# Three order tables of a four-layer graph kernel are replaced, with the sums of VectorE inside SBUF placed apart from GpSimd's long instructions

## The chip, the core and the metric

The kernel runs on one core of a Trainium2 chip. A core has five engines with queues of their own: TensorE (PE in the profile; its weight loads are PEld), VectorE (DVE), ScalarE (ACT), GpSimd (POOL) and SyncE (SP), which here issues every DMA. Each engine works through its queue in order, and engines wait for each other only through semaphores. SBUF is the memory that all of them read and write, PSUM the eight banks that TensorE writes into. The metric is the time of one execution on the device, in microseconds (us); lower is better.

## The reference

The input is 64 graphs of 128 nodes with 256 features, x [64, 128, 256], and a sparse adjacency adj [64, 128, 128]. Four layers follow each other, each with a residual and a layer norm:

```
w = adj * exp(q @ k^T); y = (w / rowsum(w)) @ v        # layer 0; q, k, v from x
x = layernorm(x + y)
h = relu(adj @ (x @ W1) + b1); h = relu(adj @ (h @ W2) + b2)
x = layernorm(x + adj @ (h @ W3) + b3)                 # layer 1
# layer 2: H = (adj != 0); conv(z, W) = Dn * (H @ (Be * (H^T @ (z @ W^T)))) + b
h = norm512(relu(conv(x, Wup))) * gamma + beta
x = layernorm(x + (conv(h, Wdown) + x))
# layer 3: 8 heads of 32, scores times (adj + adj), softmax, context, Wo
x = layernorm(x + mha(x, adj))
```

All is float32; the kernel's products with weights are made of float32r halves ("high" and "rest"), whose three products are added in PSUM.

## The kernel before

Four graphs form a group; there are 16 groups, g = 0 to 15. A group passes four stages, A (layer 0 and most of layer 1), T (the end of layer 1), B (layer 2) and C (layer 3), and several groups are in flight at a time, each in another stage. So while TensorE does the softmax products of group g - 3, it does the up projection of g - 2 and the attention of g.

What stands in what order is written in three tables. PROLOGUE lists (step, group) for each engine until the pipeline is full, SCHEDULE lists (stage, step) for one loop round, which runs 11 times, and EPILOGUE lists the rest. `run` walks through them. A step is a function of an engine: `mha_shift` of DVE is the subtraction of the row maximum from a graph's scores, and each step waits for the semaphores of what it reads. Where a step overwrites a bank or a tile that is still read, and the order doesn't already give it, there is a further wait whose count ("due") stands in a small dictionary in the step.

The steps that the prediction speaks of:
- x0's norm. DVE computes the row statistics (`x0_means`, L1306, and `x0_stats`, L1315 and L1317), GpSimd raises the variance to the power -1/2 (L1579), DVE scales (`x0_norm`, L1322), and TensorE's `gcn_ax` reads the result. x1, x2 and x3 have the same chain.
- `mha_shift3` (L1495): DVE adds the negated row maxima to graph 3's scores, both from SBUF. `mha_max` (L1491) reads the scores alone. `mha_scores` (L1486) takes the scores out of PSUM and multiplies them by adjB. ACT then takes the exponentials, GpSimd divides (`mha_div`, L1628), TensorE turns the result (`mha_turn`), ACT and DVE copy one half each (L1513 on DVE).
- `square_sum0` and `square_sum1` (L1455, L1459, L1462): DVE adds up four tiles of squares of layer 2's hidden values, from SBUF; TensorE transposes the sum in `hyper_down`.
- `mha_wo` on DVE (L1526): x3 = product in PSUM + x2. TensorE's `mha_turn3` writes its bank only after the first of these.
- `incidence` (L1407 to L1416): a compare of adjT with zero, a sum of rows, a reciprocal and a product.
- `hyper_rest` and `mha_xt` (L1301) are the "rest" halves of the up projection's and of qk's input. `rest_W...` (L1295) are those of the weights, made once. `hyper_up01` of group 0 waits for the rests of WupT, W3, Wv3T and WoT.
- On GpSimd: `up_rest` (L1612), `x_rest` (L1633), `att_t` (L1588, x plus a bias row), `x0_bias` (L1601), `x2_bias` (L1624), each a sum over 128x1024.
- On SyncE: `next_xT`, `next_x`, `gcn_3a1` (loads the adjT of the group after next), `mha_scores1` (loads the next adjB, once the masks have used the old one), `x3_norm0` and `x3_norm1` (store half of a result each, after DVE's scaling of it).

Of the kernel before, what the change touches and what calls it, by code (L numbers as in the profile page):

```python
# [55 lines left out]
def width(weights):  # L56
# [7 lines left out]
    "PE": [("set_att", 0), ("set_vec", 0), ("keep_busy2", 0), ("att_t", 0), ("att_t_rest", 0), ("keep_busy5", 0),  # L64
        ("set_down", 0), ("set_wo", 0), ("att_scores", 0), ("att_v0", 0), ("att_v1", 0), ("att_t", 1), ("att_v0", 1),
        ("att_out", 0), ("att_t_rest", 1), ("att_v1", 1), ("gram", 0), ("att_scores", 1), ("gcn_ax", 0), ("att_out", 1),
# [211 lines left out]
def build(nc, A):  # L278
# [1407 lines left out]
```

## Time and profile before

| | us |
|---|---|
| median of 3 runs | 1079.01 (1076.88 to 1079.46) |
| the profiled execution | 1078.44 |
| its span, first to last instruction | 1076.6 |
| PE busy | 1011.8 (94%) |
| DVE busy | 880.3 (82%) |
| ACT busy | 641.7 (60%) |
| POOL busy | 499.5 (46%) |
| one row maximum on DVE (L1491), mean | 1.20 |
| one copy of half a turn on DVE (L1513), mean | 0.68 |
| one load of adjT, issue to landing, median | 3.6 |

The profile is one execution. Busy is the time in which an engine had at least one instruction; the idle time ahead of an instruction is put down to the semaphore that came last. The granted clock of TensorE is given as a share of its full rate; in the profiled run it was 0.984 on average. The DMA queues moved 36 GB/s on average.

### The profile page before, as it was taken

Reading aid. Unit: us, or ns where it says so; the run is one execution under the profiler, and the core shown is the slowest. Engines: PE = TensorE matmul, PEld = TensorE weight load, DVE = VectorE, ACT = ScalarE, POOL = GpSimd, SP = SyncE. Lnnn points to the kernel's source line nnn. Section 1 sums busy time; section 2 is a strip of 40 time slices with the busy share of each in tenths; the row PEclk is TensorE's granted clock in tenths of the full one; section 3 lists DMA queues with packets and bytes.
Section 4 is the critical chain, followed back from the end, with each engine's and each line's share of the span. In section 5 each row is a group of like instructions: output and inputs, shape, how many; then the busy total and the mean of one; then the engine's idle time right before and its main releaser. Section 6 shows DMA issues by size and latency. Waiting matters only on the chain.

```text
span 1076.6 us, 21459 instructions
## 1 busy us (share of the span) xinstructions
PE 1011.8 (94%) x8252; PEld 900.9 (84%) x8252; DVE 880.3 (82%) x2252; ACT 641.7 (60%) x1739; POOL 499.5 (46%) x298
## 2 busy tenths in 40 slices
PE   7997999999999999999999999999999999988877
PEld 6896889888888988988898898888888887977665
DVE  5875798988879788888978889798888979787887
ACT  2564394755738476483846738385673838458274
POOL 3413456362734536173363626436372554418243
PEclk8998999999999999999999999999999999999988
DMA  6101010201001010010101001010100100010001
GB/s 255 40 30 40 11 51 1 80 1 50 30 21 60 11 63 8 24 57 11 69 2 50 31 21 60 11 69 2 50 31 21 59 12 21 1 41 1 1 11 50
DMA packets 15078, 39.14 MB, mean 36 GB/s; under 512 B 1792, under 2 KB 1792, under 8 KB 14848
## 3 DMA queue, kind: packets, MB, share of 16 engines
q1 hardware_dynamic: 14976, 37.77, 9.9%
q8 instruction: 65, 1.06, 0.4%
q14 instruction: 37, 0.30, 0.1%
HBM read 29.38 MB, written 8.39 MB: 35 GB/s over the span
## 4 chain that ended last, share of the span: by engine, by line
PE 64%; DVE 22%; ACT 5%; issue 4%; POOL 3%; DMA 0%; POOLq 0%; DVEq 0%; SPq 0%
PE ps L638 59%; POOL rstd L1579 3%; DVE x L1368 2%; DVE st L1306 2%; PE ps L1018 2%; DVE x L1322 2%; DVE hT L1434 2%; DVE sqs L1459 2%; DVE fT_rest L1301 2%; PE ps L947 1%; ACT aT_high L1116 1%; ACT ps L1118 1%; ACT upT L1165 1%; DVE sqs L1462 1%; PE ps L929 1%
## 5 line engine op out<-in xcount | busy, mean ns | idle before, releaser
L1628 POOL TENSOR_TENSOR pr<-pr,den 128x1024 f32<-128x1024 f32 x60 | 114.8, 1914 | 254.8 <-DVE den L1509 254.7
L1579 POOL TENSOR_TENSOR rstd<-var,neg_half 128x4 f32<-128x4 f32 (+1 forms) x84 | 83.9, 999 | 170.1 <-DVE var L1317 169.9
L1180 ACT ACTIVATE pr<-pr,mx 128x128 f32<-128x128 f32 x360 | 140.1, 403 | 7.3 <-DVE mx L1491 7.3
L1133 ACT COPY s_s<-ps 128x512 f32<-128x512 f32 x30 | 17.6, 587 | 138.6 <-PE ps L638 138.6
L1486 DVE TENSOR_TENSOR pr<-ps,adjB 128x1024 f32<-128x1024 f32 x60 | 70.5, 1216 | 20.1 <-PE ps L638 20.1
L1322 DVE TENSOR_SCALAR x<-x,mv,rstd 128x256 f32<-128x256 f32 x184 | 66.5, 418 | 22.2 <-POOL rstd L1579 21.9
L1612 POOL TENSOR_TENSOR up_rest<-upT,up_high 128x1024 fp32r<-128x1024 f32 x30 | 73.0, 2432 | 12.2 <-ACT upT L1160 12.2
L1180 ACT ACTIVATION_READ_ACCUMULATOR pr<-pr,mx 128x1 f32 x360 | 72.3, 201 | 0.0
L1174 ACT ACTIVATE qkT<-ps,biases 128x512 f32<-128x512 f32 x60 | 37.1, 689 | 57.0 <-PE ps L638 56.8
L1491 DVE TENSOR_REDUCE mx<-pr 128x8 f32<-128x1024 f32 x60 | 70.9, 1200 | 0.0
L1306 DVE BATCH_NORM_STATS2 st<-x 128x6 f32<-128x256 f32 x184 | 66.1, 412 | 0.2
L638 PE MATMUL ps<-W_high,aT_high 128*128 128x256 f32 x240 | 65.9, 298 | 0.0
L1018 PE MATMUL ps<-ident,pr 128*128 128x128 f32 x480 | 61.1, 275 | 5.1 <-DVE x L1526 5.1
L638 PE MATMUL ps<-WdownT_high,up_high 128*128 128x258 f32 x240 | 62.0, 290 | 0.7 <-DVE x L1526 0.7
L1513 DVE COPY pr<-ps 128x512 f32<-128x512 f32 x60 | 39.4, 676 | 28.2 <-PE ps L1018 28.2
L1018 PEld LDWEIGHTS ps<-ident,pr 128*128 128x128 f32 x480 | 54.0, 141 | 10.1 <-issue 7.9
L638 PE MATMUL ps<-W_rest,aT_high 128*128 128x256 f32 x240 | 62.2, 282 | 0.0
L638 PE MATMUL ps<-WdownT_rest,up_high 128*128 128x258 f32 x240 | 60.4, 283 | 0.0
L638 PE MATMUL ps<-fT_high,WupT_high 128*128 128x512 f32 x120 | 50.7, 422 | 5.4 <-DVE WoT_rest L1295 5.4
L1156 ACT ACTIVATE up_high<-ps,biases 128x512 fp32r<-128x512 f32 x60 | 41.3, 689 | 19.8 <-PE ps L638 19.7
L1301 DVE TENSOR_TENSOR fT_rest<-ps,fT_high 128x512 fp32r<-128x512 f32 x60 | 38.5, 681 | 15.1 <-ACT fT_high L1170 14.1
L1617 POOL TENSOR_TENSOR hv<-hv,neg_half 128x2 f32<-128x2 f32 x32 | 23.0, 718 | 60.2 <-DVE hv L1450 60.2
(336 smaller groups left out, 3411.0 us busy)
## 6 DMA issues: line engine op xcount, KB each, us to landing
xT<-in_xT SPq DMA_DIRECT2D x15, 512.0 KB, 3.2
x<-in_x SPq DMA_DIRECT2D x15, 512.0 KB, 3.4
out_x<-x SPq DMA_DIRECT2D x30, 256.0 KB, 2.0
adjT<-in_adjT SPq DMA_DIRECT2D x16, 256.0 KB, 3.6
adjB<-in_adj SPq DMA_DIRECT2D x15, 256.0 KB, 3.3
pr<-in_weights SPq DMA_DIRECT2D x2, 512.0 KB, 6.3
qkT<-in_weights SPq DMA_DIRECT2D x1, 1024.0 KB, 13.4
upT<-in_weights SPq DMA_DIRECT2D x1, 768.0 KB, 10.7
```

Of the source, the lines that this page charges most:

```text
L638: return pe.matmul(out, lhsT, rhs, start=(k == 0), stop=(k == n - 1))
L1018: last = pe.transpose(ps4[:, turn_bank(g, b) + k // 4, k % 4], pr_of(g)[:, b, k, :], ident[:])
L1156: act.activation(up_high_of(g)[:, f, :], ps[:, up4(g) + f, :], ACT.Relu, bias=b_up[:, f, :]).then_inc(up_high_ready, 1)
L1180: act.activation(pr_of(g)[:, b, k, :], pr_of(g)[:, b, k, :], ACT.Exp, bias=mx[ended(g)][:, b, k:k + 1], accum_out=den[ended(g)][:, b, 0, k ...
L1301: dve.tensor_tensor(part_rest[:, c, :], ps[:, bank + c, :], high_part[:, c, :], ALU.subtract).then_inc(ready, 1)
L1306: dve.bn_stats(st[norm(i, g)][:, b, :], t[:, b, :]).then_inc(norm_step[i], 1)
L1322: dve.tensor_scalar(t[:, b, :], t[:, b, :], mv[norm(i, g)][:, b, 0:1], rstd[norm(i, g)][:, b:b + 1], ALU.subtract, ALU.mult).then_inc(read ...
L1486: dve.tensor_tensor(pr_of(g)[:, b].rearrange("p (j i) n -> p j i n", i=C), ps4[:, up4(g):up4(g) + 4, 2 * bb:2 * bb + 2, :], mask, ALU.mult ...
L1491: dve.tensor_reduce(mx[ended(g)][:, b, :], pr_of(g)[:, b], AX.X, ALU.max, negate=True).then_inc(mx_ready, 1)
L1579: pool.tensor_tensor(rstd[norm(i, g)][:, bs], var[norm(i, g)][:, bs], neg_half[:, bs], ALU.pow).then_inc(rstd_ready[i], len(pairs))
L1612: pool.tensor_tensor(up_rest_of(g)[:, fs, :], upT_of(g)[:, fs, :], up_high_of(g)[:, fs, :], ALU.subtract).then_inc(up_rest_ready, 1)
L1628: pool.tensor_tensor(pr_of(g)[:, b], pr_of(g)[:, b], den[ended(g)][:, b, 1, :].unsqueeze(2).broadcast_to([P, HEADS, P]), ALU.mult).then_in ...
```

## The change

All three tables are new. No step is dropped or added. In the loop, steps of a stage moved across the round's border, so that some are listed under another stage letter (the same group of graphs all the same). Besides that the due counts of bank and tile waits are written anew for the new order. Here are the lines of the tables that hold the shift and WoT's rest, and most of the due counts:

```diff
@@ PROLOGUE, DVE
-        ("gram_scale", 2), ("gcn_ax1", 2), ("gcn_ax", 2), ("rest_WoT", 0), ("x1_stats0p", 1), ("x1_means1", 1),
...
+        ("gcn_3a1", 0), ("x1_stats0p", 0), ("rest_WoT", 0), ("x1_norm0p", 0), ("rest_WdownT", 0), ("x1_means1", 0),
...
@@ SCHEDULE, DVE
-        ("N", "x0_means0"), ("N", "x0_means1"), ("N", "x0_stats"), ("B", "mha_shift3"), ("N", "x0_norm")],
...
+        ("A", "degrees"), ("C", "mha_shift3"), ("A", "gram_scale"), ("C", "mha_div2"), ("C", "mha_turn1"),
...
@@ PE: att_t, gcn_1, gram_turn
-                        due = {(1, 1): 0, (1, 2): 0}.get((m, g), {1: 1 * g}.get(m, 0))
+                        due = {(1, 1): 0, (1, 2): 1}.get((m, g), {1: 1 * g}.get(m, 0))
...
-                due = {0: 0}.get(g, 2 * g + 2)
+                due = {1: 0, 2: 0}.get(g, 2 * g + 2)
                 if due > 0:
                     pe.wait_ge(gm_ready, due)
...
-                due = {0: 1, 1: 0, 2: 0, 3: 7, 15: 0}.get(g, 2 * g + 2)
+                due = {0: 1, 2: 5}.get(g, 0)
                 if due > 0:
                     pe.wait_ge(z2_rest, due)
@@ PE: hyper_down_high
                 pe.wait_ge(up_high_ready, HC * g + HC)
+                due = {(0, 1): 0, (0, 13): 0, (0, 14): 0, (0, 15): 0}.get((half, g), {0: 4 * g}.get(half, 0))
+                if due > 0:
+                    pe.wait_ge(prT_act, due)
@@ ACT: gram_turn, hyper_x
-                due = {2: 0, 15: 0}.get(g, 2 * g - 2)
+                due = {2: 2}.get(g, 0)
                 if due > 0:
                     act.wait_ge(hyper_done, due)
...
+                due = {1: 2, 14: 28}.get(g, 0)
+                if due > 0:
+                    act.wait_ge(v3_done, due)
@@ DVE: mha_wo
-                due = {(0, 15): 0}.get((pair, g), {0: 16 * g}.get(pair, 0))
+                due = {(0, 13): 208}.get((pair, g), 0)
                 if due > 0:
                     dve.wait_ge(out_stored[0], due)
```

The first place is x0's norm on VectorE in a loop round. Before, from the statistics of x0 (x_100) on, with `pr` the scores, `mx_124` the maxima, `dn_109` the degrees and `hT` the scaled Gram matrix:

```order
L1306 BN_STATS st_131<-x_100 128x6 x4
L1313 MEMSET held 128x1
L1315 BN_AGGR mv_139<-st_131 128x2 x4
L1317 TENSOR_REDUCE var_147<-mv_139 128x4
L1495 TENSOR_TENSOR pr<-pr,mx_124 128x1024
L1322 TENSOR_SCALAR x_100<-x_100,mv_139,rstd_155 128x256 x4
L1423 TENSOR_SCALAR dn_109<-ps 128x4
L1424 TENSOR_SCALAR dn_109<-ps 128x4
L1426 SCALAR_TENSOR_TENSOR dn_109<-ps,dn_109 128x4
L1428 RECIPROCAL dn_109<-dn_109 128x4
L1322 TENSOR_SCALAR x_odd<-x_odd,mv_140,rstd_156 128x256 x4
L1434 TENSOR_SCALAR hT<-ps,dn_109 128x128 x4
```

Now the same stretch (the line numbers are 19 higher):

```order
L1325 BN_STATS st_131<-x_100 128x6 x4
L1332 MEMSET held 128x1
L1334 BN_AGGR mv_139<-st_131 128x2 x4
L1336 TENSOR_REDUCE var_147<-mv_139 128x4
L1510 TENSOR_REDUCE mx_124<-pr 128x8
L1341 TENSOR_SCALAR x_100<-x_100,mv_139,rstd_155 128x256 x4
L1442 TENSOR_SCALAR dn_109<-ps 128x4
L1443 TENSOR_SCALAR dn_109<-ps 128x4
L1445 SCALAR_TENSOR_TENSOR dn_109<-ps,dn_109 128x4
L1447 RECIPROCAL dn_109<-dn_109 128x4
L1514 TENSOR_TENSOR pr<-pr,mx_124 128x1024
L1453 TENSOR_SCALAR hT<-ps,dn_109 128x128 x4
```

The shift went from ahead of x0's scaling to ahead of hT, the last row maximum came into its place, and x1's scaling (x_odd) left this stretch.

The second place is the squares on VectorE, later in the same round; `sqs` is their sum, `x_130` is x3, `aT_rest` a rest half. Before:

```order
L1513 COPY pr<-ps 128x512
L1386 TENSOR_TENSOR aT_rest<-ps,aT_high 128x512 x2
L1455 TENSOR_TENSOR sqs<-upT 128x512
L1526 TENSOR_TENSOR x_130<-ps,x_121 128x512
L1513 COPY pr<-ps 128x512
L1306 BN_STATS st_134<-x_130 128x6 x2
L1313 MEMSET held 128x1
L1315 BN_AGGR mv_142<-st_134 128x2 x2
L1317 TENSOR_REDUCE var_150<-mv_142 128x2
L1396 TENSOR_TENSOR ctx_rest<-ps,ctxT 128x512
L1459 TENSOR_TENSOR sqs<-sqs,upT 128x512
L1462 TENSOR_TENSOR sqs<-sqs,upT 128x512
```

Now:

```order
L1545 TENSOR_TENSOR x_130<-ps,x_121 128x512
L1332 MEMSET held 128x1
L1334 BN_AGGR mv_140<-st_132 128x2 x4
L1336 TENSOR_REDUCE var_148<-mv_140 128x4
L1532 COPY pr<-ps 128x512
L1325 BN_STATS st_134<-x_130 128x6 x2
L1332 MEMSET held 128x1
L1334 BN_AGGR mv_142<-st_134 128x2 x2
L1336 TENSOR_REDUCE var_150<-mv_142 128x2
L1341 TENSOR_SCALAR x_odd<-x_odd,mv_140,rstd_156 128x256 x4
L1474 TENSOR_TENSOR sqs<-upT 128x512
L1478 TENSOR_TENSOR sqs<-sqs,upT 128x512
```

The first sum of squares no longer stands ahead of x3's sum; all three now stand together behind x1's scaling, and the third is followed by ctx_rest.

The third place is SyncE's queue in the loop; `out_x<-x_130` is half a store of x3. Before:

```order
L602 DMA xT<-in_xT 128x1024
L617 DMA adjB<-in_adj 128x512
L606 DMA x<-in_x 128x1024
L612 DMA adjT_81<-in_adjT 128x512
L626 DMA out_x<-x_130 128x512 x2
```

Now:

```order
L604 DMA xT<-in_xT 128x1024
L628 DMA out_x<-x_130 128x512
L614 DMA adjT_81<-in_adjT 128x512
L628 DMA out_x<-x_130 128x512
L619 DMA adjB<-in_adj 128x512
L608 DMA x<-in_x 128x1024
```

The loads of adjT, adjB and x, which stood ahead of both halves of the store, now stand behind the first half or behind both.

## Rows read from the trace of the kernel before

**Rows 1.** The page, part 1: busy us (share of the span), instructions of each engine.

```profile
PE 1011.8 (94%) x8252; PEld 900.9 (84%) x8252; DVE 880.3 (82%) x2252; ACT 641.7 (60%) x1739; POOL 499.5 (46%) x298
```

**Rows 2.** Busy time by stretch: PE, PEld, DVE, ACT, POOL; PEclk; DMA.

```profile
0.00:98.73 98.73, 84.67 (x518) 75.72 (x519) 67.48 (x224) 45.40 (x97) 29.06 (x23) 0.93 0.27 99
...
225.86:861.66 635.80, 616.28 (x5122) 551.73 (x5121) 536.62 (x1371) 395.07 (x1080) 312.01 (x181) 1.00 0.10 34
...
925.00:1076.60 151.60, 126.59 (x1134) 109.21 (x1132) 118.58 (x269) 81.70 (x237) 61.12 (x40) 0.94 0.05 19
92.40:98.70 6.30, 6.30 (x18) 4.98 (x19) 2.19 (x7) 1.66 (x3) 0.00 (x0) 0.62 0.00 0
1025.60:1040.00 14.40, 13.61 (x68) 11.70 (x69) 10.81 (x18) 11.47 (x42) 5.34 (x4) 0.76 0.03 13
```

**Rows 3.** Waits of PE, whole kernel: total us, times, longest.

```profile
PE ps L638 <- DVE x L1322: 12.9, 12, 2.9
PE ps L638 <- DVE WoT_rest L1295: 5.4, 1, 5.4
PE ps L638 <- DMA pr<-in_weights: 5.4, 1, 5.4
PE ps L1018 <- DVE x L1526: 5.1, 11, 0.5
...
PE ps L638 <- DVE fT_rest L1301: 3.0, 11, 0.3
PE ps L638 <- DVE pr L1513: 2.7, 1, 2.7
PE ps L638 <- DVE att_rest L1295: 2.4, 1, 2.4
...
PE ps L638 <- DVE hT L1434: 2.1, 11, 0.2
```

**Rows 4.** The same from 225.86 to 861.66, ten loop periods.

```profile
PE ps L638 <- DVE x L1322: 8.7, 10, 0.9
```

**Rows 5.** In order of time: start us, us; POOL and DVE in a loop period.

```profile
606.27 2.41 POOL L1612 TENSOR_TENSOR up_rest<-upT,up_high 128x1024 fp32r<-128x1024 f32 x1
607.39 1.84 DVE L1455 TENSOR_TENSOR sqs<-upT 128x512 f32<-128x512 f32 x1 [0.27 <-ACT upT L1165]
608.64 2.82 POOL L1601 TENSOR_TENSOR x<-x,rows 128x1024 f32<-128x1024 f32 x1
...
657.05 1.22 DVE L1495 TENSOR_TENSOR pr<-pr,mx 128x1024 f32<-128x1024 f32 x1
657.28 1.85 POOL L1579 TENSOR_TENSOR rstd<-var,neg_half 128x4 f32<-128x4 f32 x1 [1.31 <-DVE var L1317]
```

**Rows 6.** L1455's shortest, median and longest ns; a power met by nothing.

```profile
L1455 DVE TENSOR_TENSOR sqs<-upT x15: 681/1835/2755, 106.0 to 985.5; 128x512 f32<-128x512 f32 x15
...
1006.01 1.02 POOL L1579 TENSOR_TENSOR rstd<-var,neg_half 128x4 f32<-128x4 f32 x1 [2.60 <-DVE var L1317]
```

**Rows 7.** In order of time, ACT: the two copies of aT.

```profile
661.74 1.06 ACT L1111 CAST aT_high<-ps 128x512 fp32r<-128x512 f32 x2
```

**Rows 8.** The tail in order of time: DVE's two sums of x2, PE's turn.

```profile
1019.66 1.27 DVE L1474 SCALAR_TENSOR_TENSOR x<-x_odd,ps 128x512 f32<-128x512 f32 x2
...
1025.71 0.69 PE L947 MATMUL ps<-ident,x 128*128 128x128 f32 x2 [4.74 <-DVE x L1322]
```

**Rows 9.** In order of time, PE: four matmuls of qk.

```profile
634.20 1.07 PE L638 MATMUL ps<-fT_rest,Wqk3T_high 128*128 128x512 f32 x4
```

**Rows 10.** In order of time, DVE: qk's rests, the masks of group and graph pair.

```profile
632.69 1.29 DVE L1301 TENSOR_TENSOR fT_rest<-ps,fT_high 128x512 fp32r<-128x512 f32 x2 [1.12 <-ACT fT_high L1170]
...
640.61 2.35 DVE L1486 TENSOR_TENSOR pr<-ps,adjB 128x1024 f32<-128x1024 f32 x2 [1.21 <-PE ps L638]
```

**Rows 11.** The loads of adjB, 15 of them.

```profile
DMA to landing us min/median/max: 2.7/3.3/5.3
```

**Rows 12.** The compare of the incidence: shortest, median and longest ns.

```profile
L1407 DVE TENSOR_SCALAR hT<-adjT x15: 408/417/1190, 9.2 to 888.7; 128x512 f32<-128x512 f32 x15
```

More of the change, by code:

```diff
@@ L134 @@
-    "POOL": [("x_rest", 0), ("att_t", 0), ("att_t", 1), ("x_rest", 1), ("x0_stats0p", 0), ("x0_stats1p", 0),
[7 rows of a table removed]
-    "SP": [("next_x", 2), ("next_xT", 2), ("gcn_3a1", 0), ("next_xT", 3), ("gcn_3a1", 1), ("next_x", 3),
-        ("first_adjB", 0), ("gcn_3a1", 2), ("next_xT", 4), ("mha_scores1", 0), ("next_x", 4), ("x3_norm1", 0),
-        ("x3_norm0", 0)],
+    "PE": [("keep_busy5", 0), ("set_att", 0), ("keep_busy2", 0), ("att_t", 0), ("set_vec", 0), ("att_t_rest", 0),
+        ("set_wo", 0), ("set_down", 0), ("att_scores", 0), ("att_t", 1), ("att_t_rest", 1), ("att_v0", 0),
+        ("att_v1", 0), ("att_v0", 1), ("att_out", 0), ("att_v1", 1), ("gram", 0), ("att_scores", 1), ("gcn_ax", 0),
[6 rows of a table added]
+        ("gram_turn", 1), ("gram", 2), ("hyper_x", 0), ("gcn_ax", 2), ("hyper_up01", 0), ("hyper_up01_rest", 0),
[12 rows of a table added]
+        ("hyper_out", 1), ("gram_turn", 3), ("gcn_3s1", 3), ("att_t", 4), ("gcn_3a0", 3), ("att_t_rest", 4),
+        ("mha_xt", 1), ("gcn_3a1", 3), ("mha_qk01", 1), ("mha_qk01_rest", 1), ("mha_qk2", 1), ("mha_qk3", 1)],
@@ new lines @@
+    "DVE": [("set_reps", 0), ("set_rep", 0), ("set_att", 0), ("rest_att", 0), ("incidence", 0), ("set_vec", 0),
+        ("set_down", 0), ("rest_Wv0T", 0), ("rest_W1", 0), ("set_wo", 0), ("incidence", 1), ("att_exp", 0),
+        ("att_out", 0), ("att_res1", 0), ("x0_means0", 0), ("x0_stats0p", 0), ("x0_means1", 0), ("x0_stats1p", 0),
+        ("x0_norm0p", 0), ("degrees", 0), ("x0_norm1p", 0), ("att_exp", 1), ("gram_scale", 0), ("gcn_ax", 0),
[24 rows of a table added]
+    "ACT": [("x_high", 0), ("high_att", 0), ("high_W3", 0), ("high_W2", 0), ("x_high", 1), ("att_t", 0),
+        ("high_Wv0T", 0), ("high_W1", 0), ("high_WoT", 0), ("att_t", 1), ("att_v0", 0), ("att_v1", 0), ("att_off", 0),
+        ("att_exp", 0), ("high_Wqk3T", 0), ("att_v0", 1), ("att_v1", 1), ("att_off", 1), ("att_exp", 1), ("gcn_ax", 0),
+        ("gcn_1", 0), ("gcn_2s0", 0), ("gcn_2s1", 0), ("gcn_2a", 0), ("gcn_ax", 1), ("high_WupT", 0), ("gcn_1", 1),
+        ("gcn_3s0", 0), ("gcn_3s1", 0), ("x_high", 2), ("gcn_2s0", 1), ("gcn_2s1", 1), ("high_Wv3T", 0),
+        ("high_WdownT", 0), ("gram_turn", 0), ("gcn_2a", 1), ("att_v0", 2), ("att_t", 2), ("att_v1", 2), ("att_off", 2),
+        ("att_exp", 2), ("gcn_3s0", 1), ("gcn_3s1", 1), ("gram_turn", 1), ("hyper_x", 0), ("gcn_ax", 2), ("x_high", 3),
[9 rows of a table added]
@@ L145 @@
+    "POOL": [("att_t", 0), ("x_rest", 0), ("att_t", 1), ("x_rest", 1), ("x0_stats0p", 0), ("x0_stats1p", 0),
[7 rows of a table added]
+    "SP": [("next_xT", 2), ("next_x", 2), ("gcn_3a1", 0), ("gcn_3a1", 1), ("next_xT", 3), ("first_adjB", 0),
+        ("next_x", 3), ("gcn_3a1", 2), ("next_xT", 4), ("x3_norm1", 0), ("x3_norm0", 0), ("mha_scores1", 0),
+        ("next_x", 4)],
 }
 SCHEDULE = {
[3 rows of a table removed]
[1 row of a table added]
         ("A", "att_scores"), ("C", "mha_v1"), ("B", "hyper_x"), ("A", "att_out"), ("B", "hyper_up01"),
@@ L734, in att_v @@
                     if b == 0:
-                        due = {(0, 0, 2): 1, (0, 0, 3): 5}.get((pair, b, g), 0)
+                        due = {(0, 0, 2): 1, (0, 0, 4): 7}.get((pair, b, g), 0)
                         if due > 0:
@@ L745, in att_v @@
                     elif b == 2:
-                        due = {(1, 2): 4 * g + 1}.get((pair, b), 0)
+                        due = {(1, 2, 3): 0}.get((pair, b, g), {(1, 2): 4 * g + 1}.get((pair, b), 0))
                         if due > 0:
@@ L749, in att_v @@
                     else:
-                        due = {(1, 3): 4 * g + 2}.get((pair, b), 0)
+                        due = {(1, 3, 3): 0}.get((pair, b, g), {(1, 3): 4 * g + 2}.get((pair, b), 0))
                         if due > 0:
@@ L768, in att_out @@
                     if b == 0:
-                        pass
+                        due = {(0, 3): 1}.get((b, g), 0)
+                        if due > 0:
+                            pe.wait_ge(v3_ready, due)
                     elif b == 1:
-                        due = {(1, 3): 0}.get((b, g), {1: 2 * g - 4}.get(b, 0))
+                        due = {(1, 3): 0, (1, 15): 0}.get((b, g), {1: 2 * g - 4}.get(b, 0))
                         if due > 0:
@@ L979, in mha_v @@
                     pe.wait_ge(masked_ready, due)
-                due = {(0, 0): 13, (1, 0): 14}.get((pair, g), 0)
+                due = {(1, 0): 14}.get((pair, g), 0)
                 if due > 0:
                     pe.wait_ge(res0_ready, due)
-                due = {(0, 0): 0, (0, 13): 0, (0, 14): 0, (0, 15): 0, (1, 0): 0, (1, 13): 0, (1, 14): 0, (1, 15): 0}.get((pair, g), {0: 4 * g + 15, 1: 4 * g + 16}.get(pair, 0))
+                due = {(0, 13): 31, (1, 13): 32}.get((pair, g), 0)
+                if due > 0:
+                    pe.wait_ge(res1_ready, due)
+                due = {(0, 13): 0, (0, 14): 0, (0, 15): 0, (1, 0): 0, (1, 12): 0, (1, 13): 0, (1, 14): 0, (1, 15): 0}.get((pair, g), {0: 4 * g + 15, 1: 4 * g + 16}.get(pair, 0))
                 if due > 0:
@@ L1007, in mha_turn @@
                 pe.wait_ge(pr_ready, GB * g + b + 1)
+                due = {(2, 14): 58}.get((b, g), 0)
+                if due > 0:
+                    pe.wait_ge(prT_act, due)
+                due = {(2, 14): 58}.get((b, g), 0)
+                if due > 0:
+                    pe.wait_ge(prT_dve, due)
                 due = {3: 2 * g + 1}.get(b, 0)
@@ L1013, in mha_turn @@
                     pe.wait_ge(up_ready, due)
-                due = {(1, 14): 30, (1, 15): 32}.get((b, g), 0)
+                due = {(1, 14): 30}.get((b, g), 0)
                 if due > 0:
@@ L1033, in mha_bias @@
             def mha_bias(g, pair):
-                due = {(0, 15): 61, (1, 15): 63}.get((pair, g), 0)
+                due = {(0, 15): 61}.get((pair, g), 0)
                 if due > 0:
@@ L1085, in att_t @@
                     act.wait_ge(t_done, 2 * g + m + 1)
+                    due = {(0, 0): 1}.get((m, g), 0)
+                    if due > 0:
+                        act.wait_ge(vec_ready, due)
                     act.activation(tT_of(g)[:, m, :], ps[:, low(g) + 1 - m, :], ACT.Identity, bias=t0[:, m:m + 1]).then_inc(t_ready, 1)
@@ L1150, in hyper_x @@
                 act.wait_ge(gx_done, g + 1)
+                due = {1: 2, 14: 28}.get(g, 0)
+                if due > 0:
+                    act.wait_ge(v3_done, due)
                 for c in range(C):
@@ L1156, in up_out @@
                 act.activation(up_high_of(g)[:, f, :], ps[:, up4(g) + f, :], ACT.Relu, bias=b_up[:, f, :]).then_inc(up_high_ready, 1)
-                due = {(2, 0): 1}.get((f, g), 0)
-                if due > 0:
-                    act.wait_ge(rest_ready["WoT"], due)
                 act.activation(upT_of(g)[:, f, :], ps[:, up4(g) + f, :], ACT.Relu, bias=b_up[:, f, :]).then_inc(up_ready, 1)
@@ L1516, in mha_wo @@
                 dve.wait_ge(wo_done, 2 * g + pair + 1)
-                due = {(0, 15): 0}.get((pair, g), {0: 16 * g}.get(pair, 0))
+                due = {(0, 13): 208}.get((pair, g), 0)
                 if due > 0:
                     dve.wait_ge(out_stored[0], due)
-                due = {(1, 12): 192, (1, 13): 208, (1, 14): 224}.get((pair, g), 0)
+                due = {(1, 13): 208, (1, 14): 224}.get((pair, g), 0)
                 if due > 0:
```

11 lines of the change are left out of this document (removed), and 334 rows, old and new, of tables (EPILOGUE, PROLOGUE, SCHEDULE).

## The prediction

> **What bounds the kernel now.** I read the page first, then busy times by stretch, then TensorE's waits, then the instructions around them in order of time. TensorE (PE) is busy 1011.8 us of a span of 1076.6, VectorE (DVE) 880.3 [rows 1], so at most 64.8 us can be won by order alone. The profiled execution took 1078.44, that is 1.8 more than its span and 0.6 less than the median of 1079.01. By stretch [rows 2], PE stands still for 14.1 us in the first 98.7, for 19.5 in the ten loop periods from 225.86 to 861.66 (63.58 us each) and for 25.0 in the last 151.6. Some of this can't go: 5.4 us at the start wait for the first weights [rows 3], and the last sum, norm and store stand behind the last matmul.
>
> Four waits come back in every loop period. Over the whole kernel they are, for the norm of x0 (L1322, ahead of gcn_ax) 12.9 us, for x3's sum (L1526, ahead of the fourth turn) 5.1, for fT's rest 3.0 and for hT 2.1, together 23.1 [rows 3]. In the ten periods the first is 0.87 each [rows 4] and the others by their count and longest 0.5, 0.3 and 0.2: 1.9 of the 1.95 us that PE stands still in a period.
>
> Behind two of them is one thing. At 607.39 the sum of squares L1455 starts on DVE while GpSimd (POOL) is in an up_rest that ends at 608.68 [rows 5]. It takes 1.84 us, where the shortest of its line takes 0.68 [rows 6], and it ends 0.55 us after POOL's instruction, as if it had stood until then. POOL's next, started at 608.64 while the sum still ran, takes 2.82, where the up_rest, of the same size, takes 2.41. The sum of x3 (L1526) stands behind this L1455 on DVE. At 657.05 it is the other way round: DVE starts the shift L1495 (two inputs in SBUF, 1.22 us); POOL's power L1579 is released at 657.28 and takes 1.85 [rows 5] instead of 1.02 [rows 6], and x0's scaling waits for that power, and PE for the scaling.
>
> **The change part by part.** The tables add and remove no instruction; each keeps its duration, unless two of these meet.
>
> *x0's norm in the loop.* The shift goes behind the norm and the degrees. The row maximum of graph 3, one input and 1.2 us, takes its place between variance and scaling; before it stood ahead of att_out. The power takes 1.02 instead of 1.85, 0.8 us less, and the chain starts up to 1.1 earlier since the maximum is out of its way: x0 is ready 1.9 us earlier against a wait of 0.87. Next late would be gcn_1. With 1.4 us less of waits ahead of it PE comes to it at about 662.3; ACT's two copies of aT run from 661.74 to 662.80 [rows 7], and the second is wanted 0.4 us behind the first. I put 0 to 0.4 us a period at that.
>
> *The squares.* Their sums go behind x1's norm, at a place where POOL's next instruction waits for hv, so nothing runs on POOL: 0.7 each instead of 1.84 for the first. Ahead of x3's sum there is now a turn's copy (0.7), so it ends about 1.2 us earlier, against a wait of 0.5. By my walk along the queues the squares are done 0.8 us before PE's transposes want them, the thinnest cover in the loop.
>
> *fT's rest and hT* come 1.1 us earlier with the maximum gone, against waits of 0.3 and 0.2; in front of hT x1's norm (1.35) is replaced by the shift (1.22).
>
> Loop sum, over the kernel: between 0 (every wait replaced by another) and 23.1. I take 21.0, near the upper end, as each wait has at least its own length ahead of it in the walk; 2 us stay for gcn_1.
>
> *Prologue.* PE stands 5.4 us before hyper_up01 of group 0 for WoT_rest [rows 3]. In the new table that sum stands behind gcn_3a1 of group 0, two graph stages earlier, and nothing that I see holds it. Behind the wait PE's granted clock was 0.62 for 6.3 us [rows 2]; at full clock that work takes 3.9, so 2.4 more go with the wait. att_rest moves ahead of the incidence, and PE waits 2.4 for it [rows 3]; POOL's x_rest comes later in turn, behind x's bias, so I count 1.0 of that. Together 8.8. Against it, two more rests stand ahead of group 1 on DVE. I take 8; ends 0 and 14.1, all of the stretch.
>
> *Epilogue.* The longest waits are 4.74 for x2's norm of group 15 [rows 8] and 2.7 for a turn's copy [rows 3], which stood behind a square of 2.75 us, the longest of L1455 [rows 6]. hyper_out of 15 now goes ahead of most of qk and the scores of 14, and its norm ahead of 14's masks. From the sums at 1019.66 to PE's start at 1025.71 are 6.05 us, 1.1 of them a maximum that leaves this place [rows 8]: 4.9. Meanwhile PE has 16 matmuls of 512 columns, four of which take 1.07 with a pitch of 0.23 [rows 9], 3.6 us, and the scores. About 1 us of the 4.74 is left. Behind the old wait the clock was 0.76 for 14.4 us [rows 2], which costs 3.5. With 3.7, 3.5 and 2 of the 2.7 the sum is 9.2; as the tail is a chain as much as a load, I take 8; ends -3 (a newly woven tail has new waits, as long as the turn's) and 14.
>
> The two clock terms are from the rows alone. The Trainium skill (TensorE: Matmul & The Clock Gate, Part 1) says that the gate follows how busy the array has been, with half and full rate as its only levels. The rows at 0.62 and 0.76 behind the two long waits agree, as means over both. By that rule the ends gain 5.9 us beyond their waits if these get short, and nothing if they stay long enough to drop the clock; the sum above goes by the first.
>
> *Dues* (the diff's other lines): the new ones name work that the walk has done 1 us or more before. I put them at 0, upper end 0.4 a period, as for gcn_1.
>
> *SyncE.* The next adjT is now loaded behind the store of x3's first half, adjB and x behind that of the second, which waits for x3_norm1. In the clock of a period of before: fT's rests end at 633.98 [rows 10], x3_norm1 follows until 634.6, and after two issues adjB's load starts at 635.4. Its loads land after 2.7 to 5.3 us, median 3.3 [rows 11], so at 638.7. The masks want it at 640.61, where DVE even waited 1.21 for PE [rows 10]. It is hidden with 1.9 us, and at 5.3 just so. I cost it at nothing.
>
> In sum 21 + 8 + 8 = 37. I hold back 4 for waits that the walk misses. 1078.4 - 33 = 1045.4, and with the 0.6 to the median: 1046.
>
> The skill has a rule that speaks against the change (SBUF — State Buffer, "Who interferes with whom"): not only sums of two SBUF inputs but also compares and copies in the two-port mode fight with GpSimd. The row: L1407, the compare of the incidence, takes 0.42 and once 1.19 [rows 12]. A POOL sum of 2.4 us beside it in the new order would cost DVE up to 2.4 a period by that rule; the room before the masks is about as long, so the sum stays, and the third rival below would decide earlier.
>
> **The rivals.**
> - *Only the loop gains* (0.22): the ends keep their length, as their waits move along their chains. For it: in the last stretch DVE is busy 118.6 of 151.6 us and PE 126.6 [rows 2], neither to the full. Against it: PE's longest waits there have named causes that move. 1079 - 21 + 2 = 1060.
> - *The waits move on* (0.07): in each period PE finds gcn_1's inputs, the squares' or a bank late; 1.85 becomes 1.2, over 11 periods 7 us, and the ends give 4: 1079 - 7 - 4 = 1068. For it: the thin covers of 0 to 0.8 us above.
> - *The loads come late* (0.06, the slower side): adjB waits behind x3_norm1, and each us beyond 640.6 stops the masks, then PE, in 11 periods. A landing of 10 us is 4.8 late, so 53 us, against 33 won: 1099. It decides from a landing of 8.2 us on. Against it: 5.3 is the longest so far.
> - *It doesn't do what it says* (0.03): the sums meet POOL as often as before; 1079.
>
> **How the numbers follow.** The forecast has 0.62 and its own range of 1037 to 1055; the other four hold 0.38. All but the last two are faster: faster 0.91, within 0.3% (about 3 us, what a measurement can tell from no change) 0.03, slower 0.06. The range for eight in ten goes from 1036, where the loop gives its 23 and both ends 10, to 1066, which takes in the second case and leaves out most of the third.
>
> **What would show it.** A loop period of 61.7 to 61.9 us; no power of 1.8 beside the shift; squares of 0.7; no wait of PE in the loop for x0's scaling, x3's sum or fT's rest; WoT_rest before 80 us and no stretch at 0.62 behind it; less than 1.5 us before mha_xt of 15. Wrong would be a period near 63, DVE waiting for adjB's load ahead of the masks, or ends as long as before.

## The result and the profile after

The changed kernel takes 1027.69 us (median; 1027.47 to 1028.39), the kernel before 1079.2 in the same comparison (1076.88 to 1079.46): a ratio of 0.9528, 95% interval 0.9512 to 0.9545. That is 51.5 us less. The forecast was 1046 and a range of 1036 to 1066; the gain is half as large again as forecast, and the time is outside the range. The profiled execution has a span of 1025.7.

The page, part 1, of the kernel after (busy us, share, instructions), against [rows 1]:

```profile
PE 995.3 (97%) x8252; PEld 892.4 (87%) x8252; DVE 839.7 (82%) x2252; ACT 640.0 (62%) x1739; POOL 481.2 (47%) x298
```

PE's idle time fell from 64.8 to 30.4 us, by 34.4; the prediction's parts had 31.1 of idle in them (37 less 5.9 for the clock). But PE's *busy* time fell too, by 16.5 us, with the same 8252 matmuls. Of this the prediction had only the 5.9 of the clock. The 10.2 that fell in ten loop periods, where the granted clock is 1.00 before and after, it missed.

To place the gain, one instruction per group serves as a mark, the reciprocal of the degrees on DVE. These are the marks of groups 4, 14 and 15, before and after (start us, us):

```profile
215.74 0.18 DVE L1428 RECIPROCAL dn<-dn 128x4 f32<-128x4 f32 x1
...
851.57 0.18 DVE L1428 RECIPROCAL dn<-dn 128x4 f32<-128x4 f32 x1
917.17 0.18 DVE L1428 RECIPROCAL dn<-dn 128x4 f32<-128x4 f32 x1
```

```profile
205.08 0.18 DVE L1447 RECIPROCAL dn<-dn 128x4 f32<-128x4 f32 x1
...
812.58 0.18 DVE L1447 RECIPROCAL dn<-dn 128x4 f32<-128x4 f32 x1
874.29 0.18 DVE L1447 RECIPROCAL dn<-dn 128x4 f32<-128x4 f32 x1
```

Ten periods take 607.50 instead of 635.83: 60.75 each, not 63.58. With 2.83 for each of eleven rounds:

| part | forecast | measured |
|---|---|---|
| loop, 11 rounds | 21 | 31.1 |
| prologue, to the first mark | 8 | 10.7 |
| epilogue, the rest | 8 | 9.1 |
| held back | -4 | 0 |
| sum | 33 | 50.9 |

From the mark of 14 to that of 15 the gain was 3.9; what is above 2.83 there stands with the epilogue.

Busy times of the ten periods after (columns as in [rows 2]), and PE's waits in them (total us, times, longest):

```profile
205.08:812.58 607.50, 606.10 (x5123) 549.72 (x5121) 508.60 (x1371) 394.23 (x1081) 298.43 (x180) 1.00 0.11 36
```

```profile
PE ps L640 <- ACT aT_high L1130: 0.8, 5, 0.2
```

In [rows 2] the same ten periods had 616.28 of PE busy and 19.5 of idle; now it is 606.10 and 1.4. (This view lists idle times from 0.15 us on.) Three of the four waits of [rows 3] that the prediction names are gone from the loop, those for x0, x3's sum and fT's rest. So is a fifth, for the squares, of 0.14 a period, nearly always too short for this view. The one ahead of gcn_1 is left, with 0.13 a period instead of 0.20, now for the last hT or for ACT's copy of aT, whichever comes last. DVE, busy 536.62 there, has 508.60: 2.8 us a period of VectorE's "work" was standing still. It stood without a semaphore: "engines wait for each other only through semaphores", as said further up, does not hold for these, and the profile counts such standing as busy. The squares, in order of time in a period after, against [rows 5]:

```profile
585.71 0.68 DVE L1474 TENSOR_TENSOR sqs<-upT 128x512 f32<-128x512 f32 x1
586.50 0.69 DVE L1478 TENSOR_TENSOR sqs<-sqs,upT 128x512 f32<-128x512 f32 x1
587.29 0.69 DVE L1481 TENSOR_TENSOR sqs<-sqs,upT 128x512 f32<-128x512 f32 x1
```

And x0's power with the shift of the same period, which no longer meet:

```profile
627.64 1.02 POOL L1598 TENSOR_TENSOR rstd<-var,neg_half 128x4 f32<-128x4 f32 x1
```

```profile
630.47 1.20 DVE L1514 TENSOR_TENSOR pr<-pr,mx 128x1024 f32<-128x1024 f32 x1
```

**Where PE's busy time went.** Two neighbouring groups of matmuls of PE, before and then after (start us, us):

```profile
657.70 1.05 PE L638 MATMUL ps<-bhT,hT 128*128 128x129 f32 x8
659.63 0.60 PE L638 MATMUL ps<-adjT,x 128*128 128x128 f32 x3 [0.88 <-DVE x L1322]
```

```profile
628.36 1.05 PE L640 MATMUL ps<-bhT,hT 128*128 128x129 f32 x8
629.24 1.52 PE L640 MATMUL ps<-adjT,x 128*128 128x128 f32 x12
```

From start to start this is 1.93 us before and 0.88 after: 1.05 less, for a wait shown as 0.88. In an unbroken stream the next group starts 0.17 before the last matmul of the one ahead has ended, and this overlap is lost at a stop. Means of ten periods, from the start of the matmul ahead to that of the stopped one, and from there to the next:

| PE stopped for | start to start less | of it shown as idle | the next matmul |
|---|---|---|---|
| x0 | 1.01 | 0.87 | 0.07 |
| x3's sum | 0.62 | 0.47 | 0.03 |
| fT's rest | 0.44 | 0.27 | 0.11 |
| the squares | 0.31 | 0.14 | 0.06 |

Together these are 2.64 of the 2.83, with 1.76 shown and 0.88 not: 0.19 to 0.27 a stop. Of the 512 matmuls of a period 483 start at the same distance behind the one ahead in both kernels, within 0.02, so the matmuls themselves did not get faster. The others moved by up to 0.19 either way, mostly where the new order has other neighbours, with no idle time shown. In all, the idle time of a period fell by 1.81 and the busy time by 1.02. The profile models the ends of matmuls, so how a stop is divided between idle and busy is the profile's; the starts and the times of the runs don't depend on it.

### The profile page after: what moved, and what is told of

Read it like the earlier page. It is cut to its first block, busy times and chain, and to the rows that moved or that the text cites. A ratio compares the mean times of both kernels' runs of the same rounds, so it can differ in the third digit from the quotient of the medians.

```text
span 1025.7 us, 21446 instructions
## 1 busy us (share of the span) xinstructions
PE 995.3 (97%) x8252; PEld 892.4 (87%) x8252; DVE 839.7 (82%) x2252; ACT 640.0 (62%) x1739; POOL 481.2 (47%) x298
## 3 DMA queue, kind: packets, MB, share of 16 engines
q1 hardware_dynamic: 14976, 37.77, 10.7%
## 4 chain that ended last, share of the span: by engine, by line
PE 81%; DVE 8%; ACT 6%; POOL 2%; issue 2%; DMA 1%; SPq 0%; POOLq 0%; DVEq 0%; ACTq 0%
PE ps L640 74%; PE ps L1034 4%; ACT pr L1199 2%; PE ps L954 1%; ACT up_high L1178 1%; DVE st L1325 1%; ACT upT L1179 1%; DMA rows<-in_rows 1%; DVE mx L1510 1%; POOL rstd L1598 1%; PE ps L936 1%; DVE pr L1505 1%; PE ps L867 1%; DVE x L1341 1%; DVE pr_z L1505 0%
## 5 line engine op out<-in xcount | busy, mean ns | idle before, releaser
L1598 POOL TENSOR_TENSOR rstd<-var,neg_half 128x4 f32<-128x4 f32 (+1 forms) x84 | 75.7, 905 | 91.7 <-DVE var L1336 89.7
L1607 POOL TENSOR_TENSOR x<-x,rows 128x1024 f32<-128x1024 f32 x15 | 36.0, 2400 | 81.4 <-DMA x<-in_x 71.9
L1341 DVE TENSOR_SCALAR x<-x,mv,rstd 128x256 f32<-128x256 f32 x184 | 63.8, 408 | 7.5 <-POOL rstd L1598 6.3
L640 PE MATMUL ps<-W_high,aT_high 128*128 128x256 f32 x240 | 63.7, 290 | 0.1
L640 PE MATMUL ps<-WdownT_high,up_high 128*128 128x258 f32 x240 | 61.7, 289 | 0.0
L1189 ACT CAST fT_high<-ps 128x512 fp32r<-128x512 f32 x30 | 16.1, 590 | 55.2 <-PE ps L954 55.2
```

What stands on the lines that cost most here:

```text
L640: return pe.matmul(out, lhsT, rhs, start=(k == 0), stop=(k == n - 1))
L1341: dve.tensor_scalar(t[:, b, :], t[:, b, :], mv[norm(i, g)][:, b, 0:1], rstd[norm(i, g)][:, b:b + 1], ALU.subtract, ALU.mult).then_inc(read ...
L1598: pool.tensor_tensor(rstd[norm(i, g)][:, bs], var[norm(i, g)][:, bs], neg_half[:, bs], ALU.pow).then_inc(rstd_ready[i], len(pairs))
```

## The experiments

Each is given with its period (from the same marks, ten periods) beside its time. The profile's line numbers differ a little from kernel to kernel, since the tables have other lengths.

**Does a stop cost more than it shows?** After four, or eight, steps of every group TensorE waits for its own last matmul. Of the edit, one place:

```diff
-                "gcn_2a": gcn_2a,
+                "gcn_2a": lambda g: (gcn_2a(g), pe.wait_ge(z2_done, g + 1)),
```

> The changed kernel, with TensorE made to wait for its own last matmul after four steps of every group (gcn_2a, gram, att_scores, gcn_1_rest): 64 added stops, nothing else changed. Theory (a stop of TensorE costs more than the idle time that the profile shows, because the last matmul's way through the array counts as busy): 0.20 to 0.30 us each, so 13 to 19 us, 1041 to 1047 us, and a loop period of 61.5 to 61.9 instead of 60.75, most of it as PE busy and not as PE idle. Rival (the busy time of TensorE fell in the changed kernel because its matmuls met fewer other accesses; a stop costs what it shows): idle of 0.06 or less each, at most 4 us, 1031 us.

> As drain4, and the same after four more steps (gcn_ax, gram_turn, hyper_x, the first scores of layer 3): 128 added stops. Theory: twice the cost of drain4, 26 to 38 us, 1054 to 1066 us, a straight line in the number of stops. Rival: 8 us at most, 1036 us.

Measured: drain4 1041.72 us (1040.34 to 1042.15), period 61.68; drain8 1055.24 (1054.95 to 1055.65), period 62.66. So 14.0 us for 64 stops and 27.6 for 128: 0.22 us each, on a line. This is a net price. One such stop, in drain4 and then the same place in the kernel after:

```profile
590.78 1.95 PE L640 MATMUL ps<-adjT,s_s 128*128 128x128 f32 x16
592.78 0.39 PE L640 MATMUL ps<-WdownT_high,up_high 128*128 128x258 f32 x1
```

```profile
582.47 1.95 PE L640 MATMUL ps<-adjT,s_s 128*128 128x128 f32 x16
584.18 0.37 PE L640 MATMUL ps<-WdownT_high,up_high 128*128 128x258 f32 x1
```

2.00 against 1.71 from start to start: 0.29, of which 0.05 lie between an end and a start. By the starts of matmuls in ten periods the four added places cost 0.27 to 0.32 each, 0.06 shown. TensorE then comes later to gcn_1, and the stop that was there shrinks by 0.27 a period in drain4 and goes, by 0.38, in drain8; that is the difference to 0.22. The ten periods of drain4 and drain8:

```profile
207.57:824.34 616.77, 614.33 (x5123) 550.81 (x5122) 508.58 (x1370) 395.29 (x1081) 298.44 (x180) 1.00 0.11 35
```

```profile
210.80:837.36 626.56, 621.48 (x5122) 552.28 (x5122) 507.76 (x1370) 396.16 (x1081) 298.38 (x180) 1.00 0.11 35
```

With 40 stops PE busy grows by 8.2 and idle by 1.0; with 80 by 15.4 and 3.7. The rival is out: nothing but stops was added, they cost more than they show, and four fifths of the price or more is booked as PE busy. Its other half, matmuls that met fewer accesses, is out by the 483 equal distances.

The Trainium skill has the mechanism (TensorE: Matmul & The Clock Gate, Part 2: What happens when you issue a matmul): the drain of one matmul overlaps the fill of the next, and a matmul that stands alone pays, by the page's figure, some 166 ns beyond its columns at full clock. With the 0.06 shown that makes an estimate of 0.23. The runs' times agree (0.22 net); the places themselves show somewhat more, 0.27 to 0.32. Another page of the Trainium skill (Perfetto Trace Analysis, "Identifying the Most-Contended Engine") says that matmul busy share is a poor measure of the headroom because matmuls are pipelined; here it hid 1.02 of 2.83 us.

**How much of the loop is the two-input instructions?** They are replaced by one-input row reductions with the same output (the second input is left out, so these sums, products and shifts are not computed), all five kinds of instruction or one part of them, in the order of before or (one_after) in that of after:

```diff
-dve.tensor_tensor(sqs_of(g)[:, 1, :], upT_of(g)[:, 0, :], upT_of(g)[:, 1, :], ALU.add)
+dve.tensor_reduce(sqs_of(g)[:, 1, :], upT_of(g)[:, 0, :].unsqueeze(2), AX.X, ALU.max)
...
-dve.tensor_tensor(e0_of(g)[:, b, :], e0_of(g)[:, b, :], adjT[g % 2][:, b, :], ALU.mult)
+dve.tensor_reduce(e0_of(g)[:, b, :], e0_of(g)[:, b, :].unsqueeze(2), AX.X, ALU.max)
...
-dve.tensor_tensor(pr_of(g)[:, b], pr_of(g)[:, b], mx[...].broadcast_to([P, HEADS, P]), ALU.add)
+dve.tensor_reduce(pr_of(g)[:, b], pr_of(g)[:, b].unsqueeze(3), AX.X, ALU.max)
```

> The kernel before in its own order, where five kinds of VectorE instruction with two inputs in SBUF (the three sums of squares, the product of the exponentials with adjT, the shift) are replaced by a row reduction of the same output with one input; values are wrong, sizes and order are not. Theory (two-input sums and GpSimd's instructions stop each other, and this is behind the waits of the loop): no square of over 0.8 us, the power beside the shift takes 1.0, the loop period falls from 63.58 to between 61.0 and 62.3, the kernel to 1048 to 1063 us. Rival A (any VectorE instruction is slowed beside GpSimd): squares stay at 1.8 and the time at 1079. Rival B (the order alone made the loop shorter, the stops of VectorE are hidden): squares at 0.7 but a period above 63, 1072 to 1079 us.

> The same replacement in the changed kernel. Theory: nothing is left there to win, 1025 to 1029 us and a period of 60.6 to 60.8. Rival (the new order leaves part of the stops): more than 3 us faster than 1027.7.

> The kernel before; of the five replacements of one_before only the three sums of squares (their values are then wrong). Theory (each stopped instruction costs what TensorE's wait behind it has, shown and hidden): VectorE gets 2.0 us a period back, the wait for x3's sum (0.47 and some 0.2 hidden) and that for the squares (0.13 and 0.2) go: period 62.5 to 62.8, 1067 to 1070 us. Rival (the squares have slack): above 1076.

> The kernel before; only the product of the exponentials with adjT is replaced (values wrong). This is the part that the prediction did not name. Theory: 1.02 us a period of VectorE go ahead of fT's rest and of x0's chain, the waits for fT's rest (0.29 and 0.16 hidden) and for x0 (0.87 and 0.14) go both: period 62.0 to 62.4, 1062 to 1066 us. Rival (the chain is held by something else there): 63.2 or more, 1075 to 1079 us.

> The kernel before; only the shift is replaced (values wrong). Theory: the power beside it takes 1.0 instead of 1.85, x0 comes 0.83 us earlier against a wait of 0.87: period 62.6 to 62.9, 1068 to 1071 us. Rival (the power is slow for another reason than the two inputs of the shift): 1.85 and 1079 us.

| kernel | us | period | against 63.58 |
|---|---|---|---|
| squares_one | 1063.63 | 62.59 | -0.99 |
| product_one | 1068.24 | 62.79 | -0.79 |
| shift_one | 1068.30 | 62.73 | -0.85 |
| one_before (all) | 1044.10 | 60.93 | -2.65 |
| one_after (all, new order) | 1028.86 | 60.77 | |

The three parts add up to 2.63, all together give 2.65, and the whole new order gave 2.83. By the starts of matmuls, they end different waits. squares_one ends those for x3's sum and the squares, product_one that for fT's rest and 0.14 of that for x0, shift_one 0.83 of that for x0; one_before ends all four. In shift_one the stop for x0 gets shorter but stays, and of its 0.83 all was shown: what isn't shown comes back only when a stop goes whole. So in the loop the new order is worth nearly nothing beyond keeping these instructions apart, and in the new order nothing of them is left. one_before came out 4 us below what was expected of it, squares_one 3 below, product_one 2 above. The squares in one_before, shortest, median and longest ns, against [rows 6] (and the same line of the kernel after below it):

```profile
L1455 DVE TENSOR_REDUCE sqs<-upT x15: 675/686/687, 107.4 to 953.5; 128x512 f32<-128x512 f32 x15
```

```profile
L1474 DVE TENSOR_TENSOR sqs<-upT x15: 681/686/1614, 95.0 to 943.0; 128x512 f32<-128x512 f32 x15
```

The product of the exponentials with adjT, which the prediction did not name, was stopped too. Its longest one before, and what GpSimd did at that time in a period:

```profile
L1359 DVE TENSOR_TENSOR e<-e,adjT x60: 276/279/1121, 30.7 to 904.3; 128x128 f32<-128x128 f32 x60
```

```profile
647.72 1.90 POOL L1628 TENSOR_TENSOR pr<-pr,den 128x1024 f32<-128x1024 f32 x1 [13.70 <-DVE den L1509]
```

The four products start at 648.64 and take 1.73 together; GpSimd's division ends at 649.62. The first of them takes 1.12, the others 0.28. A short instruction waits out the rest of a long one. In sum the products lose 0.86 us a period (1.95 against 1.09 after), not the 1.02 of the expectation.

**Is one move enough?** The shift and the maximum moved alone in the old order, the shift moved back in the new one:

```diff
 # shift_before (before, DVE, loop); shiftmax_before also moves ("B", "mha_max3") ahead of x0_norm
-("A", "degrees"), ("T", "x1_norm"), ... ("N", "x0_stats"), ("B", "mha_shift3"), ("N", "x0_norm")
+("A", "degrees"), ("C", "mha_shift3"), ("T", "x1_norm"), ... ("N", "x0_stats"), ("N", "x0_norm")
 # shift_after (after, DVE, loop)
-("C", "mha_max3"), ("A", "x0_norm"), ("A", "degrees"), ("C", "mha_shift3"),
+("C", "mha_max3"), ("C", "mha_shift3"), ("A", "x0_norm"), ("A", "degrees"),
```

> The kernel before; in the loop the shift of graph 3 goes from ahead of x0's scaling to behind the degrees, nothing else moves. Theory: the wait for x0's scaling (0.87 a period, and some 0.2 that the profile counts as busy) goes, as the shift (1.2) and the power's extra 0.8 leave the chain; the shift now stands ahead of x1's scaling and hT, whose own wait (0.2) may grow. Period 62.5 to 62.8 instead of 63.58, 1066 to 1070 us, no power of over 1.1 beside a shift. Rival (the wait moves to hT behind the shift): 63.2 to 63.6, 1075 to 1079 us.

> As shift_before, and the last row maximum goes from ahead of att_out to between x0's variance and its scaling, as in the changed kernel. Theory: the rest of the wait for x0 and those for fT's rest go too; what stays are the squares, x3's sum and the product of the exponentials: period 62.0 to 62.5, 1061 to 1067 us. Rival (order of the chain without the squares brings nothing more): as shift_before, within 3 us of it.

> The changed kernel; in the loop the shift goes back ahead of x0's scaling, now with the last maximum ahead of it. Theory (what this move is worth is 1 us a period, and it can be read from either kernel): x0 comes 1.2 us later and 0.8 more by the power; period 61.4 to 62.2, 1035 to 1043 us. Rival (in the changed kernel the chain of x0 has slack for it, the gain came from elsewhere): 60.7 to 61.0, 1028 to 1031 us.

shift_before took 1081.64 us, 3 more than before (ratio 1.0035, 1.0025 to 1.0046; period 63.91): the theory fell, the rival was right and more so. shiftmax_before took 1074.24 (63.07), 4 less than before and 7 above what was expected; shift_after 1036.75 (61.44), 9.1 more than the changed kernel, as the theory had it. PE's waits in ten periods of shift_before and of shift_after:

```profile
PE ps L573 <- DVE hT L1369: 13.4, 10, 1.3
```

```profile
PE ps L629 <- DVE x L1330: 8.6, 10, 0.9
```

In shift_before the wait for x0 is gone, and PE waits 1.3 for hT, because x1's scaling (1.4) and the shift (1.2) now both stand ahead of it. The changed kernel had moved x1's scaling away. The same move is worth -0.33 us a period in one order and +0.69 in the other.

**The ends.** WoT's halves moved in the old prologue; the new kernel with the old tail; and WoT with the one-input instructions:

```diff
 # wot_before (before, prologue); ACT's ("high_WoT", 0) goes behind ("high_W1", 0) likewise
-("gcn_ax", 2), ("rest_WoT", 0), ("x1_stats0p", 1)
+("gcn_3a1", 0), ("rest_WoT", 0), ("x1_means1", 0)
 # old_tail: EPILOGUE of every engine in the order of before, with its due counts
```

> The kernel before; in the prologue alone WoT's high half (ScalarE) goes behind that of W1 and its rest (VectorE) behind gcn_3a1 of group 0. Theory: the wait of 5.39 us goes and with it the stretch at a clock of 0.62 (2.4 us): 7 to 8 us less, 1071 to 1072 us. Rival (the next rest half, or hyper_rest of group 0, ends the wait nearly as late): within 3 us of before.

> The changed kernel up to the end of its loop, and behind it what is left of every engine's work in the order of the kernel before. Theory (the new tail is worth about what the prediction gave it, 8, and the 3.9 of the eleventh round belong to the loop): 8 to 11 us slower than the changed kernel, 1035 to 1039 us, with the wait for x2's norm of group 15 back at 4 us or more. Rival (most of the tail's gain came with the loop and its stops, not with its own order): less than 4 us, 1028 to 1031 us.

> one_before (the five kinds of VectorE instruction with one input in place of two, values wrong) and wot_before in one kernel. Theory (the two act in different stretches and add): 1044.1 - 7.1 = 1037, within 2 us; what is then left to the changed kernel, some 9 us, is the tail's order and the small waits of the prologue. Rival (in the prologue the two share a wait): 1040 or more.

wot_before: 1071.54, 7.1 less, as expected. old_tail: 1037.80, 10.1 more than the changed kernel (by the profiled execution, which was its fastest, 8.0: 2.9 in the eleventh round and 5.2 behind it), with this wait of PE back:

```profile
PE ps L879 <- DVE x L1266: 4.7, 1, 4.7
```

locks_wot: 1036.45, where 1037 was the sum. So the parts add: 34.2 us for the two-input instructions (26.5 of them in ten periods, the rest in the eleventh round and the ends), 7.1 for WoT, and 8.8 for what is left to the changed kernel; the sum is 50.1 against 51.5, while the medians of before were between 1076.8 and 1079.5 over these comparisons. By the marks of locks_wot and of the changed kernel that rest (9.0 in the profiled executions) is 1.4 in the first stretch, 2.1 in the ten periods, 1.3 in the eleventh round and 4.2 behind it. old_tail's 8 to 10 can't be set against it as they are: the old tail brings its two-input meetings back too, which the 34.2 hold already. The prologue's own share was not run apart.

Of wot_before's gain 5.6 lie ahead of the first mark and 1.5 behind the loop. In the first stretch the wait of 5.4 and the low clock behind it are gone, but PE now waits 1.5 for the squares there.

**SyncE's queue** put back (with waits on the stores that this order needs):

```diff
-("N", "next_xT"), ("C", "x3_norm0"), ("T", "gcn_3a1"), ("C", "x3_norm1"), ("C", "mha_scores1"), ("N", "next_x")
+("N", "next_xT"), ("C", "mha_scores1"), ("N", "next_x"), ("T", "gcn_3a1"), ("C", "x3_norm0"), ("C", "x3_norm1")
```

> The changed kernel with SyncE's loop queue as before (the loads of adjB, x and adjT ahead of both halves of the store), and with the waits on the stores that this needs. Theory (the loads have cover in either place): within 3 us of 1027.7. Rival (the stores now free x3's tile later, or the loads in the new place cost nothing only by luck of the landing): over 3 us away.

1031.81, 4.1 more, outside the expected 3. The period is 60.76, the same: in the loop it costs nothing. In the profiled execution, the slowest of the four, with a span 5.3 longer, the loss is in the first stretch (0.9) and behind the loop (0.7 in the eleventh round, 3.5 after it, where the granted clock fell to 0.72 in 999 to 1004 us); which of the added waits or loads makes it is open.

**Can the last stop be won back?** One stop of the loop is left after, ahead of gcn_1. The expectation of gram_first takes it as 0.04, behind the last hT. That is one period of the ten; in the other nine it shows 0.13 to 0.16, and in six of the ten ACT's copy of aT comes last.

```diff
 # gram_first (after, DVE, loop)
-("C", "mha_shift3"), ("A", "gram_scale"),
+("A", "gram_scale"), ("C", "mha_shift3"),
 # last_stop: also, on ACT
-("C", "mha_exp2a"), ("A", "gcn_ax"),
+("A", "gcn_ax"), ("C", "mha_exp2a"),
```

> The changed kernel with hT's scaling ahead of the shift in the loop. There TensorE has one stop left in a period, ahead of gcn_1, shown as 0.04 us of idle, behind the fourth hT. Theory (a stop costs about 0.2 us more than it shows): the period falls by 0.2 to 0.25 from 60.75, and the kernel by 2 to 3 us to 1024.7 to 1025.7. Rival (a stop is worth its idle time): 0.04 a period, 0.5 us, not to be told from 1027.7; or the later shift makes a new wait for graph 3: 1028 or more.

> As gram_first, and on ScalarE the two copies of aT go ahead of four exponentials of graph 2, since in gram_first the same stop now waits for the first of these copies (0.16 shown). Theory (a stop costs about 0.2 us more than it shows): the stop goes, the period falls by 0.2 to 0.25 to 60.5, the kernel to 1024 to 1025.5 us. Rival (a stop is worth what it shows, or a new one comes for the exponentials or the turn's copies behind them): 1026.5 us or more.

gram_first: 1027.19 (1027.04 to 1027.77), period 60.74: no change that can be told; the stop stayed, in nine periods of ten, now always for ACT's copy (0.13 to 0.17 shown). The test was of the wrong input, not of the price. last_stop: 1032.69, period 61.12, slower. There the stop did go: from the start of the turns to that of gcn_1 it is 0.38 us a period less, for 0.13 that had been shown, in line with the price of a stop. But a new one came, in ten periods:

```profile
PE ps L622 <- DVE pr L1514: 5.1, 10, 0.5
```

The turn's copies now come late behind the shift, for 0.76 a period from start to start (0.76 - 0.38 is the 0.37 by which the period grew). No version here beats the changed kernel by more than the measurement can tell.

## Why the prediction was wrong

**The step that failed** is the loop's term: "Loop sum, over the kernel: between 0 (every wait replaced by another) and 23.1. I take 21.0". The cause of the waits was right: three of the four named went, and the idle time came nearly as predicted, 18.1 us in ten periods, where 21 over eleven rounds makes 19.1. A part of that is luck: 1.4 of the 18.1 are the squares' wait, which the prediction took for covered, while gcn_1's stayed. But 23.1 was no upper end, because the term prices a stop at its shown idle time. A stop of TensorE that goes is worth 0.19 to 0.27 us more, which the profile counts as busy. In ten periods PE busy fell by 10.2 us, 8.8 of them at the four stops that went, and with it the loop gave 31.1. The same error stands in the opening sentence, that "at most 64.8 us can be won by order alone".

**What it left out beside.** It sized only the first square (1.84 against 0.68) and the power. The second square (1.57 median) and the products (0.86 a period) met GpSimd as well. The product's part is 0.79 of the 2.83, and it was to be seen in the trace: shortest 276, longest 1121 ns. It did not make the sum wrong by itself, since the idle waits were counted in full anyway, but it made the cover look thinner than it is, and behind it stood the rival *the waits move on* and the 4 us held back. In the ten periods nothing was lost to new waits.

**Point by point.** A period of 61.7 to 61.9: wrong, 60.75. No power of 1.8 beside the shift, squares of 0.7, no wait in the loop for x0, x3's sum or fT's rest: right. WoT's rest before 80 us: right, at 66.28, and no stretch at 0.62 behind it (1.00 in 92.4 to 98.7). Its term of 5.4 + 2.4 measured 7.1 in wot_before, 5.6 of it ahead of the first mark. The prologue's other term, 1.0 for att_rest, was too small: that wait went from 2.4 to 0.3, and the clock behind it, which the prediction had not looked at, was 0.69 and 0.63 in 10 to 20 us before (means between its full 2.4 and half of 1.2 GHz), against 1.00 and 0.74 after. There matmuls that only fill now stand ahead of the first weights, and att_rest comes sooner; which of the two raised the clock was not run apart:

```profile
10.00:15.00 5.00, 2.62 (x14) 2.01 (x15) 4.54 (x11) 0.00 (x0) 2.90 (x3) 0.69 1.02 416
15.00:20.00 5.00, 5.00 (x16) 3.94 (x15) 0.00 (x0) 1.56 (x3) 1.99 (x1) 0.63 0.99 412
```

```profile
10.00:15.00 5.00, 4.69 (x29) 3.73 (x27) 4.50 (x7) 0.36 (x1) 3.97 (x2) 1.00 1.03 417
15.00:20.00 5.00, 4.36 (x15) 3.19 (x15) 1.78 (x5) 2.79 (x5) 4.37 (x3) 0.74 0.98 410
```

The epilogue's 8 measured 9.1. Of the 4.74 ahead of mha_xt of 15 nothing is left, where the prediction kept about 1 and promised less than 1.5; the longest waits of the tail are now two of 1.55, ahead of mha_xt of 13 and of a turn:

```profile
902.99 1.41 PE L954 MATMUL ps<-ident,x 128*128 128x128 f32 x8 [1.55 <-DVE x L1341]
...
973.60 1.09 PE L954 MATMUL ps<-ident,x 128*128 128x128 f32 x8
```

The loads of adjB in the loop land after 2.6 to 3.9 us and DVE stands 3.25 for PE ahead of the masks, so the slower rival never came near. The stop ahead of gcn_1 is the one left in the loop, as the 2 us kept for it said, but it is worth 0.38 a period, 4.2 in eleven rounds. The compare of the incidence, which the prediction feared beside a GpSimd sum, takes 0.42 in every period of the loop; once, at 116.97 in the prologue, it takes 1.44 and ends 0.29 after GpSimd's instruction.

## What to carry to other kernels

Where TensorE is the bound and its matmuls follow each other closely, count its stops, not only its idle time: each added one cost 0.27 to 0.32 us here at its place with 0.06 shown. Read them from start to start of the same group of matmuls in two places. A VectorE instruction with two inputs in SBUF whose longest time is far above its shortest is standing behind GpSimd: list min and max of every such line before sizing any one of them. And price a moved instruction with what then stands beside it: the same move was worth 0.69 us a period in one order and cost 0.33 in the other.

## What the runs showed that was not expected

- The three kinds of stopped instruction were worth 0.99, 0.79 and 0.85 us a period apart and 2.65 together, so nearly additive, although each frees VectorE at another place in one chain. They ended different waits of TensorE.
- An instruction of 128 elements a partition (0.28 us) stood up to 1.12 behind a GpSimd instruction of 1.90.
- TensorE's own busy time fell by 16.5 us for the same matmuls, and 483 of the 512 of a period kept their distance to the one ahead.
